# A graph network on one core: relation weights in four 32-column groups, another order of the set-up, and the last value rows between the first scores

## What is computed

```python
scores = jnp.einsum('ehd,ehd->eh', q[src], k[dst])          # per edge and head, softmax over the edges of src
attn   = ex / segment_sum(ex, src)[src]
out    = segment_sum(attn[:, :, None] * v[dst], src) @ wo + bo
...
w   = jnp.einsum('rb,bio->rio', att, basis)                 # rgcn: 2 relations from 30 bases of 512 x 512
msg = sigmoid(x[col] @ gate_w[r]) * x[col] @ w[r]           # r = edge_type
agg = segment_sum(msg, row) + x @ root + bias
```

## Time and profile before

| | |
|---|---|
| median of three runs | 2523.33 us (2522.43 to 2525.38) |
| the profiled execution's own time | 2519.68 us |
| its span | 2517.6 us |
| TensorE busy | 2348.3 us (93%) |
| VectorE busy | 1644.2 us (65%) |
| ScalarE busy | 1140.9 us (45%) |
| DMA moved | 189.53 MB in 57250 packets |

### The profile page before, as it was taken

The page is one execution under the profiler, slowest core; times in us unless marked ns, Lnnn a source line. Parts: engine busy times, 40 slices in busy tenths (PEclk is TensorE's granted clock), DMA queues, the critical chain, the costliest instruction groups (busy, mean ns, idle before and its releaser), DMA issues.

```text
span 2517.6 us, 36458 instructions
## 1 busy us (share of the span) xinstructions
PE 2348.3 (93%) x13669; PEld 1975.0 (78%) x13669; DVE 1644.2 (65%) x3638; ACT 1140.9 (45%) x1804; POOL 530.5 (21%) x397
## 2 busy tenths in 40 slices
PE   3989997679999999899999899999999999999999
PEld 1665553368998888899889899888899888877887
DVE  7489995364887764687765588775378776244234
ACT  2216663233776333577433477533377734332321
POOL 1200000000665000466100266300066500000000
PEclk9999998889999999999999999999999999999999
DMA  8936669731111310210320110310111132031013
GB/s 181 234 74 137 133 136 249 208 121 49 31 31 35 105 38 19 61 41 1 100 67 19 49 41 21 100 59 26 49 31 31 34 106 79 1 100 51 1 59 103
DMA packets 57250, 189.53 MB, mean 75 GB/s; under 512 B 6789, under 2 KB 7237, under 8 KB 53245
## 3 DMA queue, kind: packets, MB, share of 16 engines
q1 hardware_dynamic: 52119, 177.94, 26.2%
q10 hardware_dynamic: 4966, 9.32, 1.2%
HBM read 155.15 MB, written 32.07 MB: 74 GB/s over the span
## 4 chain that ended last, share of the span: by engine, by line
PE 79%; DVE 7%; DMA 4%; issue 4%; ACT 4%; SPq 1%; POOL 0%; ACTq 0%; DVEq 0%
PE PS L1020 9%; PE PS L1048 9%; PE PS L788 7%; PE PS L942 6%; PE PS L944 6%; PE PS L943 6%; PE PS L1034 6%; PE PS L928 4%; PE PS L839 4%; PE PS L932 4%; PE PS L929 4%; DMA basis_t<-in_L_gnn_basis_dram 4%; PE PS L1174 4%; PE PS L1184 4%; PE PS L820 2%
## 5 line engine op out<-in xcount | busy, mean ns | idle before, releaser
L768 POOL TENSOR_SCALAR prob<-prob,inv_den 125x1000 f32<-125x1000 f32 x160 | 444.4, 2778 | 0.0
L788 PE MATMUL PS<-basis_t,att_z 120*128 120x512 f32 x512 | 259.9, 629 | 46.6 <-DMA basis_t<-in_L_gnn_basis_dram 46.5
L756 POOL TENSOR_TENSOR rstd<-var_eps,neg_half 125x2 f32<-125x2 f32 x45 | 33.4, 743 | 1030.7 <-DVE var_eps L1537 1030.7
L1378 ACT ACTIVATE prob<-prob,neg_max 125x1254 f32<-125x1254 f32 x160 | 215.5, 1347 | 71.8 <-DVE neg_max L1872 71.8
L1867 DVE CUSTOM_DVE_ANT_0 prob<-PS,sbias 125x1254 f32<-125x1254 f32 x160 | 233.0, 1456 | 8.9 <-issue 6.1
L1048 PE MATMUL PS<-pT_hi,v_hi 125*128 125x250 f32 x800 | 236.0, 295 | 0.0
L1886 DVE TENSOR_TENSOR pT_lo<-PS,pT_hi 125x1000 fp32r<-125x1000 f32 x160 | 191.1, 1194 | 52.1 <-ACT pT_hi L1395 52.1
L1048 PE MATMUL PS<-pT_lo,v_hi 125*128 125x250 f32 x800 | 224.0, 280 | 0.0
L1048 PE MATMUL PS<-pT_hi,v_lo 125*128 125x250 f32 x800 | 222.4, 278 | 0.0
L1034 PE MATMUL PS<-ident,prob 125*125 125x125 f32 x1600 | 201.1, 273 | 7.1 <-DVE pT_lo L1889 7.1
L1034 PEld LDWEIGHTS PS<-ident,prob 125*125 125x125 f32 x1600 | 195.9, 188 | 13.8 <-issue 9.1
(11 more groups left out here) (324 smaller groups left out, 5785.1 us busy)
## 6 DMA issues: line engine op xcount, KB each, us to landing
basis_t<-in_L_gnn_basis_dram SPq DMA_DIRECT2D x32, 1920.0 KB, 13.2
sbias<-score_bias SPq DMA_DIRECT2D x40, 548.6 KB
adj<-adj SPq DMA_DIRECT2D x20, 546.9 KB
w_lo_raw<-in_L_gnn_m_w_dram SPq DMA_DIRECT2D x8, 1024.0 KB, 7.0
score_bias<-cnt SPq DMA_DIRECT2D x10, 548.6 KB
adj<-count_t SPq DMA_DIRECT2D x10, 546.9 KB
xc<-x_lat SPq DMA_DIRECT2D x12, 448.0 KB
x_first<-x_lat SPq DMA_DIRECT2D x10, 448.0 KB
```

The lines of the kernel that those rows point to most:

```text
L768: pool.tensor_scalar(prob[u % 3][:, 0:SPLIT], prob[u % 3][:, 0:SPLIT], inv_den[0:T, u % 4:u % 4 + 1], None, ALU.mult)\
L788: g = pe.matmul(PS[:, 6 + n % 2, :], att_z[n // (NW // 2)][:, 15 - row:143 - row], basis_t[load % 3][:, q, :], start=(row == 0), stop=(row ...
L1378: act.activation(prob[u % 3][:], prob[u % 3][:], ACT.Exp, bias=neg_max[0:T, u % 4:u % 4 + 1], scale=SCALE, accum_out=den[0:T, u % 4:u % 4 ...
```

## The change

Relation steps now come in fours, one per 32-partition quarter of the PSUM bank, with a window of `att_z` that is 32 columns wide; the four of one `turn` share that window. A load brings, for 16 rows, two out of each four, in pieces of 4 KB instead of 16. The table `rel_w` gets another order, so that the 16 rows are stored in one contiguous piece. 32 steps stand before sorting, 56 in 14 of the 20 batches (`QUADS_SORT`), 148 after 37 of the 98 groups (`QUADS_COUNT`), and 20 after the first five tiles (`QUADS_BIAS` works out to 5). All 32 loads stand ahead of the bias stage in SP's list. SP also issues the node stores, after load 6. `wk`, `x_first` and `wq` are loaded after load 26, `wv` and `x_second` at tile 4. The last pair's value rows are made between the first scores.

```diff
-        att_z = [m(f"att_z{l}", [4 * B, 15 + 128]) for l in range(2)]
+        att_z = [m(f"att_z{l}", [4 * B, 24 + 32]) for l in range(2)]
...
-        STEPS_FIRST, STEPS_RANK = 2 * QL, 4 * QL
-        STEPS_COUNT = STEPS_FIRST + STEPS_RANK + 3 * SORT_BATCHES // 2
-        STEPS_BIAS = STEPS_COUNT + NG
-        LOADS_BEFORE = STEPS_BIAS // QL + 3
-        STEPS_TILE = 10
+        STEPS_FIRST, STEPS_RANK = 2 * QL, 2 * QL
+        QUADS_SORT = [b for b in range(SORT_BATCHES) if b % 10 not in (0, 3, 6)]
+        QUADS_COUNT = [n for n in range(NG) if n % 8 in (1, 4, 7)]
...
+        QUADS_BIAS = (16 * NW - STEPS_FIRST - STEPS_RANK) // 4 - len(QUADS_SORT) - len(QUADS_COUNT)
+        rel_w = rel_w.rearrange("l a b d -> l (a b) d").rearrange("l (q r i) d -> l q r i d", r=R, i=4)
...
-                rows = (basis1, basis2)[l].rearrange("b (i q) d -> (b i) q d", q=Q)
-                sp.dma_start(basis_t[n % 3][:], rows[:, q0:q0 + QL, :]).then_inc(basis_in[n % 3], 16)
-
-            for n in range(LOADS_BEFORE):
+                rows = (basis1, basis2)[l].rearrange("b (i q k t) d -> (b i) q k t d", i=4, k=4, t=4)
+                t = q0 % 16 // 4
+                sp.dma_start(basis_t[n % 3][:].rearrange("p (k t) d -> p k t d", k=4),
+                             rows[:, q0 // 16, :, t:t + 2, :]).then_inc(basis_in[n % 3], 16)
+
+            for n in range(NL):
                 load_bases(n)
...
+                if n == 6:
+                    for p in range(NP):
+                        sp.wait_ge(h0_ready, p + 1)
+                        for r0, r1 in ROWS:
+                            sp.dma_start(pair_rows(x_lat, p)[r0:r1, :, :], x0[p][r0:r1, :, :]).then_inc(x_stored[p].sem, 16)
+                if n == NL - 6:
                     for p in range(NP):
                         wait(sp, x_stored[p], "setup", 0)
...
-                if t == 8:
+
+            for t in range(NT):
+                sp.wait_ge(count_t_done, t + 1)
+                if t == max(QUADS_BIAS - 1, 0):
                     sp.wait_ge(basis_used, NL)
                     load_mods(0, ((s1_w, s1_b), (b1_w, b1_b)))
...
-                    g = pe.matmul(PS[:, 6 + n % 2, :], att_z[n // (NW // 2)][:, 15 - row:143 - row],
-                                  basis_t[load % 3][:, q, :], start=(row == 0), stop=(row == 15))
+                    turn, quad = row // 4, row % 4
+                    g = pe.matmul(PS[32 * quad:32 * (quad + 1), 6 + n % 2, :],
+                                  att_z[n // (NW // 2)][:, 24 - 8 * turn:56 - 8 * turn],
+                                  basis_t[load % 3][:, 2 * quad + turn % 2, :], start=(turn == 0), stop=(turn == 3))
...
-                relation_steps(step, 1)
-                step += 1
+                if n in QUADS_COUNT:
+                    relation_steps(step, 4)
+                    step += 4
...
                 for i in range(4 * NP):
                     for a in range(2):
                         scores(i, a)
+                        if i == 0:
+                            value_rows(NP - 1, a)
...
-                for r in range(R):
-                    act.dma_start(rel_w[l, r, :, :].rearrange("(i q) d -> i q d", q=Q)[:, q0:q0 + 16, :],
-                                  w_out[n % 4][64 * r:64 * (r + 1), :]).then_inc(w_stored[n % 4], 16)
+                act.dma_start(rel_w[l, q0:q0 + 16, :, :, :].rearrange("q r i d -> (q r i) d"), w_out[n % 4][:])\
+                    .then_inc(w_stored[n % 4], 16)
...
+            def steps_follow(steps):
+
+                steps_done[0] += steps
+                if steps_done[0] >= 16 * (steps_done[1] + 1) + 4:
+                    store_weights(steps_done[1])
+                    steps_done[1] += 1
...
                     for a in range(2):
                         if i >= 1:
                             pT_high(i - 1, a)
+                        if i == 0:
+                            value_high(NP - 1, a)
                         exponentials(i, a)
...
                         masking(i, a)
+                        if i == 0:
+                            value_low(NP - 1, a)
                         if i >= 1:
                             pT_low(i - 1, a)
```

More of the change, by code:

```diff
@@ L488, in load_x @@
                     sp.dma_start(x[r0:r1, :, :], pair_rows(x_lat, p)[r0:r1, :, :]).then_inc(x_loaded[p].sem, 16)
-            weights = [(rel_w[l, 0, :, :], rel_w[l, 1, :, :], root) for l, root in enumerate((root1, root2))]
             def load_r(l, n):
-                sp.dma_start(wr_raw[n][:], weights[l][n].rearrange("(c p) d -> p c d", p=128)).then_inc(w_in[n].sem, 16)
+                w = rel_w[l, :, n, :, :] if n < R else (root1, root2)[l].rearrange("(c p) d -> p c d", p=128)
+                sp.dma_start(wr_raw[n][:], w).then_inc(w_in[n].sem, 16)
             def load_input(p):
@@ L567, in _ @@
                     sp.dma_start(score_bias[t, r0:r1, :], cnt0[t % 2][r0:r1, :]).then_inc(sbias_stored[t % 2], 16)
-                for n in BASES_AT.get(t, ()):
-                    load_bases(n)
             wait(sp, w_lo_done, "setup", 0)
@@ L825, in _ @@
                     hidden(fw2, z1, z2_ps)
-                fill = 1 + b % 2
-                relation_steps(step, fill)
-                step += fill
+                if b in QUADS_SORT:
+                    relation_steps(step, 4)
+                    step += 4
             pe.wait_ge(cond_hi, 1)
@@ L853, in _ @@
                 g.then_inc(csumT_ps, 1)
-                steps = min(STEPS_TILE, 16 * NW - step)
-                relation_steps(step, steps)
-                step += steps
+                if t < QUADS_BIAS:
+                    relation_steps(step, 4)
+                    step += 4
             assert step == 16 * NW
@@ L974, in _, with value_rows @@
                 last = lay + 1 == LAYERS
+                def value_rows(p, a):
+                    qkv_bank_free(pe, v_lo_done, 2 * p + a, lay)
+                    rows(qkv_bank(v_lo_done, 2 * p + a), a, yT_hi[p % 2], yT_lo[p % 2], wv_hi, wv_lo,
+                         bv3).then_inc(v_ps.sem, 1)
                 for p in range(NP):
@@ L1003, in _ @@
                         wait(pe, bv_ready, lay, 0)
-                    for a in range(2):
-                        qkv_bank_free(pe, v_lo_done, 2 * p + a, lay)
-                        rows(qkv_bank(v_lo_done, 2 * p + a), a, yT_hi[s], yT_lo[s], wv_hi, wv_lo,
-                             bv3).then_inc(v_ps.sem, 1)
                     if p + 1 < NP:
+                        for a in range(2):
+                            value_rows(p, a)
                         attention_transposed(lay, p + 1, 1)
@@ L1267, in _ @@
             node_relu()
-            store_weights(2)
-            store_weights(3)
+            steps_done = [STEPS_FIRST + STEPS_RANK, 2]
+            def steps_follow(steps):
[3 more added lines that the diff above has]
+                    steps_done[1] += 1
+            for b in range(13):
+                if b in QUADS_SORT:
+                    steps_follow(4)
             act.wait_ge(z2_ps, 1)
@@ L1275, in _ @@
             z.then_inc(cond_hi, 1)
+            for b in range(13, SORT_BATCHES):
+                if b in QUADS_SORT:
+                    steps_follow(4)
             for n in range(NG):
@@ L1283, in _ @@
                     .then_inc(group_out, 1)
-                if (STEPS_COUNT + n) % 16 == 0:
-                    store_weights((STEPS_COUNT + n) // 16 - 1)
-            for p in range(NP):
-                wait(act, x_stored[p], "setup", 0)
+                if n in QUADS_COUNT:
+                    steps_follow(4)
             act.wait_ge(count_added, NG)
-            WEIGHTS_AT = {0: 10, 2: 11, 4: 12, 5: 13, 7: 14, 8: 15}
             for t in range(NT):
@@ L1313, in _ @@
             for i in range(4):
-                act.wait_ge(w_stored[i], 32 * (NW // 4))
+                act.wait_ge(w_stored[i], 16 * (NW // 4))
             for i in range(2):
```

66 lines of the change are left out of this document (35 added, 31 removed).

## The result

| | before | after |
|---|---|---|
| median, four runs of each on the same chip | 2523.86 us | 2438.46 us |
| lowest to highest | 2522.43 to 2525.38 | 2437.36 to 2439.17 |
| the profiled execution's own time, span | 2519.68, 2517.6 us | 2438.79, 2437.1 us |
| TensorE, VectorE, ScalarE busy | 93, 65, 45% | 91, 68, 47% |
| DMA packets | 57250 | 67362 |

The changed kernel takes 0.9661 of the time (95% interval 0.9644 to 0.9678). It is faster by 85.4 us in the medians and by 80.5 in the spans, since the profiled execution of before was 4.2 us faster than the median of its four runs, and that of after 0.3 us slower than its own. The forecast was 2452, so the gain is 14 us larger than foretold.

The account below looks back on a forecast made before the run. Each set-up stage had its own limit: basis loads, TensorE in sorting, VectorE in counting, late loads in biases; TensorE filled the layers. Terms -24.5 + 4.5 + 5 + 4 - 52 - 1 - 7 = -71 us gave 2452, range 2415 to 2493.

Parts of the forecast that it names:

- The price of a group: Four relation steps on TensorE, half overlapped, take 2.2 us, between bounds of 0.86 and 3.44; chance of overlapping pairs 0.42.
- Start of sorting: Set-up before sorting: only four basis loads stand ahead, so sorting starts at 67.9 us instead of 92.4; -24.5 us.
- Sorting: Sorting stage: +4.5 us for TensorE's batches and groups of four, +5 for a late basis load; +9.5 in all.
- the late load 7: In sorting, basis load 7, issued behind the node stores, lands near 113 us while TensorE wants it at 107.6; +5 us.
- Counting: Counting stage: TensorE needs 189 us, VectorE 192; it fits with nothing to spare and interlocks imperfectly; +4 us.
- Biases: Bias stage to first modulation: tiles wait for the bias store, 9.63 us each; 87 us against 139; -53 with earlier loads.
- First scores: First scores of four layers: moved value rows fill TensorE's gaps, 1.8 us a layer; -7 us.
- All four at once: Rival for groups in sorting and counting: four steps overlap fully, 1.0 us a group; 2439 us; chance 0.18.
- Faster loads: Rival for basis loads: 4 KB pieces reach 350 GB/s instead of 203; 2434 us, or 2421 with full overlap; chance 0.18.
- batch at 68: Sign that the forecast is right: the first sorting batch starts near 68 us.
- modulation near 445: Sign that the forecast is right: the first modulation, where the layers begin, comes near 445 us.
- tiles 9.6 us apart: Sign that the forecast is right: bias-stage tiles start 9.6 us apart, VectorE waiting for `score_bias` stores.

Follow-up runs that it names:

- e9_all: Changed kernel with four edits: `count` cleared earlier, logarithm added first, exponential's table loaded early, basis loads 0 and 1 ahead of the coefficient loads; 2407.1 us.
- e1_zero_first: Changed kernel, but GpSimd clears `count` before it multiplies `z`, not after; 2424.4 us.
- e12_two_stores: Changed kernel with two store issues for 16 rows of relation weights instead of one; 2440.1 us.
- e6_exp_table: Changed kernel with a one-element exponential on ScalarE before the last pair's value rows of layer 0, so the table loads there; 2434.7 us.

## Why the prediction was right, and where not

**The price of a group** was the step that failed: I took 2.2 us from "instructions begin in order, the second half of one runs beside the first half of the next". It is 1.00, and 3.55 on one quarter: the two arrangements that ran lie near the two ends of my bounds (0.86 and 3.44), and none at the middle that I took. I had put more chance on it than on full overlap (0.42 against 0.18) without a row for it. The Trainium skill (TensorE: Matmul & The Clock Gate, Part 3, on packing small matmuls) had it near full overlap, and its figure was the better guide; here the overlap is 3.55 / 1.00, so 3.55 times for four. The passages between forms cost little: 0.14 us between 0.86 and 1.00 within the group, and 0.20 in front of it in sorting (2.85 against 2.65), 0.11 in counting (1.21 against 1.10). A drain at each change of mode (the Trainium skill, TensorEngine Tiling (Array Packing), Key Properties) would have to fit into these; no run shows whether it is one. The miss was cheap, since VectorE sets the pace in both stages: it is the 4 us that I gave counting.

**Start of sorting**, -24.5: right in place, load 3 sets it (63.86 against 63.49), and in size (67.42 against 67.9) partly by luck. I had two groups at 2.2 us behind that load, and they took 1.8 each only because TensorE ran at 1.2 GHz there (granted clock 0.50). In e9_all, at 46.75, two groups behind a load took 1.9 us together, at a clock of 1.00.

**Sorting**, +9.5 against +13.4: near in size by luck, wrong in both reasons. TensorE's groups and the late load 7 cost nothing, since VectorE sets the pace, 3.9 us a batch. What cost was the memset (9 of the 13.4 us, by e1_zero_first; the rest is VectorE's pace), which I had not costed because the diff doesn't touch it. It was moved all the same, in relation to VectorE's work.

**Counting**, +4 against -0.9: the term was for groups of 2.2 us. With groups of 1.00 TensorE is busy 162 of 194 us; VectorE's 1.96 us a group holds, as foretold.

**Biases**, -53 against -55.7: the mechanism was right, the tile waits for the store of `score_bias`. Its period is 8.4 us and not the 9.63 of the one row I had, because a tile starts 4.1 us after the store's issue (392.81 to 396.89) and not 5.3 (502.04 to 507.31), with one longer tile of 11.0 (405.02 to 416.06), where `wv` and `x_second` are loaded.

**First scores**, -7 against -12.3 for all that follows the modulation, 10.8 of it up to the last exponential: the waits gave 2.1 us a layer in layers 1 to 3, against 1.8. What the term lacked is the clock: TensorE was at 1.2 GHz for 3 us behind the fifth score's wait, 1.3 us a layer, and isn't now. In layer 0 the table load and the clock, which falls there now, take all of it back. The last 1.5 us lie behind the last exponential, where traces differ by more without any cause in the code.

**All four at once**, the rival with a chance of 0.18: its price held, and its 2439 is the measured time. That is luck in part. It had sorting at +3, which came to +13.4, and made that good with the layers (-7, measured -12.3), the biases (-53, measured -55.7) and the 4.9 us by which the medians lie further apart than the spans.

**Faster loads**, a rival: fell. 213 GB/s against 204 over 25 to 60 us, load 3 at 63.86 against 63.49, and no time with the old pieces.

What would show it: all but one of the signs came (batch at 68, 1.96 us a group, waits for `score_bias`, modulation near 445, no wait before second and third score in three layers); "tiles 9.6 us apart" did not.

## What to carry to other kernels

Small matmuls that write different 32-partition quarters ran at once here and cost together about what one costs (1.00 against 0.86 us); on one quarter they cost four times that, which ate all that the rest of this change gains. A change that frees one engine moves the others' work against each other: list what the off-path engines do in the stretch that becomes critical, and not only what the diff touches. Where a double buffer is freed by a store, do what feeds the store first; and watch how many issues stand in front of work that others wait for.

## What the hardware did that I had not expected

GpSimd can hold a VectorE instruction for as long as its own lasts. In the changed kernel and its variants a VectorE TENSOR_SCALAR from SBUF to SBUF of 0.3 or 0.4 us lasted to the end of a GpSimd instruction: 13.4 us beside the multiplication and the memset behind it, 10.7 beside the memset, 3.0 us beside the moved memset, 2.9 beside the multiplication. Not every instruction was held. VectorE's masking, a custom instruction that reads PSUM and SBUF, was not by GpSimd's 2.78 us (all 160 of them lasted 1.45 to 1.47 us), nor was a TENSOR_SCALAR of one column from SBUF to SBUF:

```profile
1003.19 1.46 DVE L1898 CUSTOM_DVE_ANT_0 prob<-PS,sbias 125x1254 f32<-125x1254 f32 x1
...
1003.40 2.78 POOL L771 TENSOR_SCALAR prob<-prob,inv_den 125x1000 f32<-125x1000 f32 x1
...
1004.69 0.15 DVE L1902 TENSOR_SCALAR has_edge<-row_max 125x1 f32<-125x1 f32 x1
```

The Trainium skill (SBUF — State Buffer, Who interferes with whom) states such a rule: the two share a pair of ports under an exclusive lock, `tensor_scalar` can take both, and whoever comes second is blocked for the whole instruction. The traces agree for the large TENSOR_SCALARs: the one of e1_zero_first began at 70.43, in the middle of the memset, and ended with it. In the changed kernel the record of the held one begins 0.03 us before GpSimd's (78.42 and 78.45), too close to tell who came first. By this rule the memset would have been a term of the prediction.

Four DMA issues in a row on ScalarE took 2.5 to 4.9 us in counting, while the one of the changed kernel takes 0.33 and two in e12_two_stores took 1.1 together; an issue among the four lasted up to 2.7 us. Why they take so much longer than four single ones, no run here tells apart from the transfers' load at that time.

The clock behind a short wait is not settled. In e6_exp_table the first five scores start at the same distances in all four layers, with the same waits; it fell behind them in layer 0 (0.56 from 566 to 569 us) and stayed full in layers 1 to 3.
